# A low-pass image layer on one core: rows and columns streamed together, x read twice

## The chip, the cores and the metric

The kernel runs on one core of a Trainium2 chip. The number that counts is the device time of one execution in microseconds (us). The chip's engines are called PE (TensorE, matmuls), DVE (VectorE), ACT (ScalarE), POOL (GpSimd) and SP (SyncE, which only issues DMAs here). They run side by side, each in the order of its own program, and wait for each other by semaphores.

## What is computed

```python
xs = jnp.einsum('bhwc,dc->bhwd', x, W1) + b1        # x: 16 x 64 x 64 x 768 f32, W1: 192 x 768
xs = jax.nn.gelu(xs, approximate=False)
# fft_low: 2-D FFT over h and w, keep frequencies -16..15 of both, inverse, real part, abs
xs = fft_low(xs)
xs = jnp.einsum('bhwd,cd->bhwc', xs, W2) + b2       # W2: 768 x 192
return x + xs
```

The low pass is a real filter matrix along W, the same along H, and a small correction for the asymmetric frequency, called the corner: it depends on four sums per channel and has period 4 along both axes. Then comes the absolute value.

## The kernel before

Sixteen images pass one after the other. An image has 32 tiles of 128 pixels (two rows each); a *pair* is two tiles, so it has 16 row pairs. A *unit* is four 128x128 blocks of x; a row pair has three units (`UPP`), and a *step* has three parts j = 0, 1, 2.

**Row part of a step** (pair q). PE transposes unit n + 2 (`transpose_unit`, L385), ACT copies it rounded to `xt_hi` (L521), DVE subtracts to `xt_lo` (L640); PE multiplies unit n by W1 (`mm1_unit`, L400 and L401). At j = 1 and j = 2 DVE adds the two PSUM halves and the bias (`hid_sum` L651, `hid_pre` L656). One step later ACT does Gelu twice (L528, L529), DVE the low part (`hid_lo`, L662), PE filters along W (L411 to L413), ACT stages the result in `filt` (L535), and SP writes it to the DRAM tensor `filtered_rows` (L300). POOL accumulates the sums for the corner from `hid` (L760 to L765).

**H phase.** When all rows of an image are written, SP reads them back by columns (L310, L317: pieces of 512 and 256 bytes, into the space of `xt_hi` and `xt_lo`, and into `cols_b`), and PE runs four chunks (`filter_h_chunk`): three banks of 512 columns each, into which first a corner matmul (L435, L443) and then four fp32 filter matmuls (L437, L445) go. ACT and DVE empty the banks with an absolute value into `ya` and `yb` (L543, L680). During the phase no mm1 runs, since its buffers hold the columns.

**Column part of a step** (pair r, of the image before). ACT splits the pair into high parts (`split_hi_pair`, L553 to L559), DVE into low parts (L686, L693), both one step ahead of their use; PE computes four output halves of 384 columns, five matmuls each (`out_half`, L462 to L472), in three PSUM banks in turn; DVE adds each half to x (L702), which has stayed in SBUF as `xs` (the last eight tiles as `x_tail`, copied by ACT, L565). SP stores groups of four tiles and loads the next image's into the freed space (L275 to L295).

**Order.** `steps` sets what runs in a step: in a turn of the loop 8 steps have a column pair alone, 4 have both, 12 have a row pair alone, three more a column pair alone, then follow the H phase and the last column pair. In a column step DVE does `add_half` and the splits after the row part's work of the same j. `turns` writes image 0 out, loops over the rest (`Fori(1, IMAGES)`: 14 jumps back), and ends with the last image's columns. PSUM has eight banks: `ps_xt` 0, 1; `ps_h` 2, 3; `ps_f` 4; `ps_o` 6, 7, 5.

## Time and profile before

| | |
|---|---|
| median of 3 runs | 2669.03 us (2663.34 to 2671.54) |
| the profiled execution, its span | 2680.7 us |
| PE busy | 2549.4 us (95%) |
| DVE busy | 1833.9 us (68%) |
| ACT busy | 1350.4 us (50%) |
| POOL busy | 397.9 us (15%) |
| DMA, mean over the span | 509 MB, 190 GB/s |
| mean granted clock of PE, of full speed | 0.975 |

The rows below come from this one profiled execution. In the table of stretches each row has the stretch in us from the start of the span, its length, then for each engine the time it was busy and (x) how many instructions, the granted PE clock as a share of full speed, the DMA engines' busy share, and GB/s. In the timelines a row has the start in us, the duration in us, engine, line, operation, what is written <- what is read, shapes, how many such instructions are merged (x), and in brackets the idle time ahead of it with what ended it. PE is pipelined: the next matmul starts before the record of the last one ends, so spacings are read from start to start. fp32 matmuls leave two records each.

### The profile page before, as it was taken

Reading aid. Unit: us, or ns where it says so; the run is one execution under the profiler, and the core shown is the slowest. Engines: PE = TensorE matmul, PEld = TensorE weight load, DVE = VectorE, ACT = ScalarE, POOL = GpSimd, SP = SyncE. Lnnn points to the kernel's source line nnn. Section 1 sums busy time; section 2 is a strip of 40 time slices with the busy share of each in tenths; the row PEclk is TensorE's granted clock in tenths of the full one; section 3 lists DMA queues with packets and bytes.
Section 4 is the critical chain, followed back from the end, with each engine's and each line's share of the span. In section 5 each row is a group of like instructions: output and inputs, shape, how many; then the busy total and the mean of one; then the engine's idle time right before and its main releaser. Section 6 shows DMA issues by size and latency. Waiting matters only on the chain.

```text
span 2680.7 us, 53277 instructions
## 1 busy us (share of the span) xinstructions
PE 2549.4 (95%) x16864; PEld 2485.4 (93%) x16864; DVE 1833.9 (68%) x3980; ACT 1350.4 (50%) x3077; POOL 397.9 (15%) x500
## 2 busy tenths in 40 slices
PE   8899898998999989899998999989999899998999
PEld 7799898998989989899898999989999899998999
DVE  6487575775758757587675766757667576675767
ACT  5355454554545545455454545545455454554544
POOL 1102021020211202112020120201202012020120
PEclk9899999999999999999999999999999999999999
DMA  6474664746647466474665846558455584555845
GB/s 207 106 252 138 201 242 114 264 129 200 240 114 261 131 198 242 114 273 129 204 230 129 282 116 215 208 135 298 103 211 202 140 300 99 207 204 145 299 102 221
DMA packets 342566, 509.48 MB, mean 190 GB/s; under 512 B 78418, under 2 KB 210770, under 8 KB 342228
## 3 DMA queue, kind: packets, MB, share of 16 engines
q1 hardware_dynamic: 342228, 505.31, 59.8%
q8 instruction: 171, 2.80, 0.4%
q14 instruction: 167, 1.37, 0.2%
HBM read 253.60 MB, written 251.66 MB: 188 GB/s over the span
## 4 chain that ended last, share of the span: by engine, by line
PE 83%; DMA 6%; SPq 4%; issue 3%; DVE 2%; ACT 2%; DVEq 0%; ACTq 0%
PE ps L400 22%; PE ps L385 12%; PE ps L401 10%; PE ps L472 6%; PE ps L462 6%; PE ps L463 5%; PE ps L469 5%; PE ps L466 5%; DMA xt_hi<-filtered_rows 4%; PE ps L437 3%; SPq L317 2%; PE ps L411 2%; PE ps L445 2%; DMA filtered_rows<-filt 2%; PE ps L413 2%
## 5 line engine op out<-in xcount | busy, mean ns | idle before, releaser
L400 PE MATMUL ps<-w1s,xt_hi 128*128 128x384 f32 x3072 | 980.2, 374 | 0.0
L521 ACT ACTIVATE xt_hi<-ps 128x512 fp32r<-128x512 f32 x768 | 457.7, 598 | 697.8 <-PE ps L385 674.5
L401 PE MATMUL ps<-w1s,xt_lo 128*128 128x192 f32 x3072 | 772.3, 251 | 0.0
L640 DVE TENSOR_TENSOR xt_lo<-ps,xt_hi 128x512 fp32r<-128x512 f32 x768 | 529.8, 691 | 282.4 <-ACT xt_hi L521 279.6
L702 DVE TENSOR_TENSOR xs<-ps,xs 128x384 f32<-128x384 f32 x1024 | 564.5, 556 | 210.9 <-PE ps L472 159.8
L401 PEld LDWEIGHTS ps<-w1s,xt_lo 128*128 128x128 f32 x3072 | 588.0, 191 | 0.0
L400 PEld LDWEIGHTS ps<-w1s,xt_hi 128*128 128x128 f32 x3072 | 578.8, 188 | 0.0
L472 PE MATMUL ps<-w2b_hi,ob 128*128 128x384 f32 x1024 | 357.0, 349 | 42.7 <-DVE ob L693 42.7
L763 POOL TENSOR_TENSOR diff<-hid 128x192 f32<-128x192 f32 x240 | 232.2, 967 | 1016.8 <-ACT hid L529 1016.8
L462 PE MATMUL ps<-w2a_hi,oa_hi 128*128 128x384 f32 x1024 | 361.3, 353 | 20.8 <-DVE xs L702 19.7
L385 PE MATMUL ps<-ident,xs 128*128 128x128 f32 x2304 | 344.1, 273 | 11.2 <-DMA xs<-x_dram 10.6
L463 PE MATMUL ps<-w2a_lo,oa_hi 128*128 128x384 f32 x1024 | 352.7, 344 | 0.0
L466 PE MATMUL ps<-w2b_lo,ob 128*128 128x384 f32 x1024 | 351.7, 343 | 0.6 <-ACT ob L559 0.6
L469 PE MATMUL ps<-w2a_hi,oa_lo 128*128 128x384 f32 x1024 | 352.2, 344 | 0.0
L385 PEld LDWEIGHTS ps<-ident,xs 128*128 128x128 f32 x2304 | 274.6, 140 | 23.3 <-issue 7.6
L472 PEld LDWEIGHTS ps<-w2b_hi,ob 128*128 128x128 f32 x1024 | 197.7, 193 | 56.0 <-DVE ob L693 51.8
L553 ACT ACTIVATE oa_hi<-ya 128x256 fp32r<-128x256 f32 x256 | 106.1, 414 | 279.0 <-PE ps L472 276.9
L462 PEld LDWEIGHTS ps<-w2a_hi,oa_hi 128*128 128x128 f32 x1024 | 197.7, 193 | 31.2 <-issue 29.0
L680 DVE TENSOR_SCALAR ya<-ps 128x512 int32<-128x512 int32 x64 | 44.3, 692 | 234.2 <-PE ps L437 234.2
L466 PEld LDWEIGHTS ps<-w2b_lo,ob 128*128 128x128 f32 x1024 | 198.0, 193 | 1.0 <-ACT ob L559 0.9
L463 PEld LDWEIGHTS ps<-w2a_lo,oa_hi 128*128 128x128 f32 x1024 | 198.2, 194 | 0.2
L469 PEld LDWEIGHTS ps<-w2a_hi,oa_lo 128*128 128x128 f32 x1024 | 197.6, 193 | 0.2
(62 smaller groups left out, 3051.3 us busy)
## 6 DMA issues: line engine op xcount, KB each, us to landing
out_dram<-xs SPq DMA_DIRECT2D x127, 1536.0 KB, 9.3
xs<-x_dram SPq DMA_DIRECT2D x80, 1536.0 KB, 7.2
filtered_rows<-filt SPq DMA_DIRECT2D x256, 192.0 KB, 2.0
x_tail<-x_dram SPq DMA_DIRECT2D x32, 1536.0 KB, 8.5
xs<-x_dram SPq DMA_DIRECT2D x32, 768.0 KB, 6.3
xt_hi<-filtered_rows SPq DMA_DIRECT2D x64, 256.0 KB, 5.1
cols_b<-filtered_rows SPq DMA_DIRECT2D x128, 128.0 KB, 5.4
xt_lo<-filtered_rows SPq DMA_DIRECT2D x64, 256.0 KB, 6.4
```

The costliest lines, as they stand in the source:

```text
L385: ins = nc.tensor.transpose(ps_xt[n % 2][:, b * P:(b + 1) * P], x_tile(t)[:, k * P:(k + 1) * P], ident[:])
L400: nc.tensor.matmul(ps_h[t % 2][:, 0:2 * D], hi, w1s[:, k, :], start=k == 0, stop=False)
L401: ins = nc.tensor.matmul(ps_h[t % 2][:, D:2 * D], lo, w1s[:, k, 0:D], start=False, stop=k == KC - 1)
L462: nc.tensor.matmul(o, a_hi, w2a_hi[:, n], start=True, stop=False)
L463: nc.tensor.matmul(o, a_hi, w2a_lo[:, n], start=False, stop=False)
L466: nc.tensor.matmul(o, b1, w2b_lo[:, n], start=False, stop=False)
L469: nc.tensor.matmul(o, a_lo, w2a_hi[:, n], start=False, stop=False)
L472: nc.tensor.matmul(o, b, w2b_hi[:, n], start=False, stop=True).then_inc(s_o, 1)
L521: nc.scalar.activation(xt_hi[:, n % XT_SLOTS, :], ps_xt[n % 2][:], ACT.Copy).then_inc(s_xhi, 1)
L640: nc.vector.tensor_tensor(xt_lo[:, n % XT_SLOTS, :], ps_xt[n % 2][:], xt_hi[:, n % XT_SLOTS, :].bitcast(F32), ALU.subtract).then_inc(s_xlo, 1)
L702: nc.vector.tensor_tensor(x_half, out_bank(u)[:, 0:HALF], x_half, ALU.add).then_inc(s_add, 1)
L763: nc.gpsimd.tensor_tensor(diff[:], hid[:, q % 2, 0, :], hid[:, q % 2, 1, :], ALU.subtract).then_inc(s_diff, 1)
```

## The change

x is no longer kept in SBUF. It is loaded twice: by row pairs into `xa` (four slots, loaded three steps ahead) for the row part, and by column pairs into `xc` (eight slots, four steps ahead) for the addition and the store; output is stored per column pair. A *column pair* is two positions w, each with all 64 h of both halves of W, so 128 pixels a column. `filtered_rows` has room for all images and is read in eight groups of four columns (`read_cols`, 3072 bytes a piece). Global step s does row pair s, and the column pair whose output halves come 19 steps later (`OUT`); filter H, `y_pair` and the splits of a column pair are done one step ahead of its output halves (`FILTER_H` = 18). There is no H phase any more. The corner is a 128x24 table (three tiny matmuls once per image into the filter's bank, copied by DVE) which `y_pair` adds, repeated along H, when it empties the bank; ACT then takes the absolute value six times: high parts as before, and `y_abs` for the low parts. POOL packs the 64 rear channels of the columns into `cols_b` in every second step. `ps_o` has two banks, 6 and 7. The loop is `Fori(2, IMAGES - 1)`: 12 jumps back.

The core of the diff (of the functions that only got other names for their arguments nothing is shown):

```diff
+PAIRS = 16
...
+AHEAD = 2
 XT_SLOTS = 4
+XA_SLOTS, XA_LEAD = 4, 3
+XC_SLOTS, XC_LEAD = 8, 4
+CHUNKS, COL_SLOTS = 8, 4
+LATE = 1
+FILTER_H = PAIRS + 2
+OUT = FILTER_H + 1
+STORE = OUT + 1
+READ_COLS = FILTER_H - 1
...
+        def stage(i, s, lag):
+            k, r = divmod(s - lag, PAIRS)
+            if whole(i) and not 0 <= i + k < IMAGES:
+                return None
+            return i + k, r
...
+            turn(0, PAIRS)
+            turn(1, PAIRS)
+            with eng.Fori(2, IMAGES - 1) as i:
+                turn(i, PAIRS)
+            turn(IMAGES - 1, PAIRS)
+            turn(IMAGES, PAIRS)
+            turn(IMAGES + 1, STORE - PAIRS)
...
+                    if at := stage(i, s, -XA_LEAD):
+                        load_xa(*at)
+                    if at := stage(i, s, STORE):
+                        store(*at)
+                    if (at := stage(i, s, READ_COLS)) and at[1] == 0:
+                        all_rows_written(at[0])
+                    if at := stage(i, s, OUT - XC_LEAD):
+                        load_xc(*at)
+                    if (at := stage(i, s, READ_COLS)) and at[1] % 2 == 0:
+                        read_cols(at[0], at[1] // 2)
+                    if at := stage(i, s, LATE):
+                        write_rows(*at)
...
+            def filter_h_pair(m, r):
+                c = r // 2
+                if r % 2 == 0:
+                    until(pe, s_cols[c % COL_SLOTS], 16 * CHUNKS // COL_SLOTS, m, 16 * (c // COL_SLOTS + 1))
+                    until(pe, s_cols_b, CHUNKS, m, c + 1)
+                until(pe, s_y, PAIRS, m, r)
+                if r == 0:
+                    until(pe, s_corner, 1, m, 1)
+                col = cols[:, c % COL_SLOTS, 2 * (r % 2):2 * (r % 2) + 2, :]
+                for v in range(2):
+                    nc.tensor.matmul(ps_y[:, v * P:(v + 1) * P], col[:, v, 0:P], fh[:], start=v == 0, stop=False)
+                col_b = cols_b[:, c % COL_SLOTS, 2 * (r % 2):2 * (r % 2) + 2, :].rearrange("p v d -> p (v d)")
+                nc.tensor.matmul(ps_y[:, 2 * P:3 * P], col_b, fh[:], start=False, stop=True).then_inc(s_h, 1)
+            def out_half(m, r, u):
+                v, f = divmod(u, 2)
+                until(pe, s_add, 4 * PAIRS, m, 4 * r + u - 1)
+                o = ps_o[u % 2][:, 0:HALF]
...
+                a_hi, a_lo, b, b1h = (t[:, r % 2, v, :] for t in (oa_hi, oa_lo, ob, ob1))
+                if u == 0:
+                    until(pe, s_hi, PAIRS, m, r + 1)
...
+                if u == 0:
+                    until(pe, s_alo, PAIRS, m, r + 1)
...
+                if u == 0:
+                    until(pe, s_blo, PAIRS, m, r + 1)
...
+                        if at := stage(i, s, 0):
+                            transpose_unit(at[0], UPP * at[1] + j + AHEAD)
+                            mm1_unit(at[0], UPP * at[1] + j)
+                        if j == 1 and (at := stage(i, s, LATE)):
+                            filter_w_pair(*at)
+                        if j == 2 and (at := stage(i, s, FILTER_H - 1)) and at[1] == 0:
+                            corner_sums(at[0])
+                        if at := stage(i, s, OUT):
                             for u in OUT_HALVES[j]:
...
+            def split_hi_pair(m, r):
+                until(act, s_o, 4 * PAIRS, m, 4 * (r - 1))
+                until(act, s_y, PAIRS, m, r + 1)
+                until(act, s_blo, PAIRS, m, r - 1)
+                yr, hi, hi1 = y[:, r % 2, :, :], ob[:, r % 2, :, :], ob1[:, r % 2, :, :]
+                nc.scalar.activation(oa_hi[:, r % 2, :, :], yr[:, 0:2, :], ACT.Abs)
+                nc.scalar.activation(hi[0:DB, 0, :], yr[0:DB, 2, :], ACT.Abs)
+                nc.scalar.activation(hi[DB:P, 1, :], yr[DB:P, 2, :], ACT.Abs)
+                nc.scalar.activation(hi1[0:DB, 0, :], yr[0:DB, 2, :], ACT.Abs)
+                nc.scalar.activation(hi1[0:DB, 1, :], yr[DB:P, 2, :], ACT.Abs)
+                nc.scalar.activation(y_abs[:, r % 2, :, :], yr, ACT.Abs).then_inc(s_hi, 1)
...
+                        if j == 1 and (at := stage(i, s, FILTER_H)):
+                            split_hi_pair(*at)
...
+                until(dve, s_y, PAIRS, m, 0)
+                nc.vector.tensor_copy(corner[:].rearrange("p g n -> p (g n)"), ps_corner[:]).then_inc(s_corner, 1)
+            def y_pair(m, r):
+                until(dve, s_h, PAIRS, m, r + 1)
+                until(dve, s_blo, PAIRS, m, r - 1)
+                if r == 0:
+                    until(dve, s_corner, 1, m, 1)
+                table = corner[:].rearrange("p g (a n) -> p g a n", a=1).to_broadcast([P, 3, 16, 8])
+                nc.vector.tensor_tensor(y[:, r % 2, :, :].rearrange("p g (a n) -> p g a n", n=8),
+                                        ps_y[:, 0:3 * P].rearrange("p (g a n) -> p g a n", g=3, n=8), table,
+                                        ALU.add if r % 2 == 0 else ALU.subtract).then_inc(s_y, 1)
+            def split_lo_pair(m, r):
+                until(dve, s_hi, PAIRS, m, r + 1)
+                yr, hi, o = y_abs[:, r % 2, :, :], oa_hi[:, r % 2, :, :], ob[:, r % 2, :, :]
+                nc.vector.tensor_tensor(oa_lo[:, r % 2, :, :], yr[:, 0:2, :], hi.bitcast(F32), ALU.subtract).then_inc(s_alo, 1)
                 for v, (own, other) in enumerate(((slice(0, DB), slice(DB, P)), (slice(DB, P), slice(0, DB)))):
+                    ins = nc.vector.tensor_tensor(o[other, v, :], yr[own, 2, :], o[own, v, :].bitcast(F32), ALU.subtract)
                 ins.then_inc(s_blo, 1)
+            def add_half(m, r, u):
+                until(dve, s_o, 4 * PAIRS, m, 4 * r + u + 1)
+                n = r % XC_SLOTS
+                if u == 0:
+                    until(dve, s_xc[n], 16 * PAIRS // XC_SLOTS, m, 16 * (r // XC_SLOTS + 1))
+                x_half = xc[:, n, u // 2, u % 2 * HALF:(u % 2 + 1) * HALF]
+                nc.vector.tensor_tensor(x_half, ps_o[u % 2][:, 0:HALF], x_half, ALU.add).then_inc(s_add, 1)
...
+                        if at := stage(i, s, 0):
+                            xt_lo_unit(at[0], UPP * at[1] + j + AHEAD)
+                        if j == 0 and (at := stage(i, s, LATE)):
+                            hid_lo_pair(*at)
+                        if j >= 1 and (at := stage(i, s, 0)):
+                            hid_sum(at[0], 2 * at[1] + j - 1)
+                            hid_pre(at[0], 2 * at[1] + j - 1)
+                        if whole(i) and i == 0 and (s, j) in set_up_at:
+                            set_up_at[s, j]()
+                        if j == 2 and (at := stage(i, s, FILTER_H - 1)) and at[1] == 0:
+                            corner_copy(at[0])
+                        if at := stage(i, s, FILTER_H):
+                            if j == 1:
+                                y_pair(*at)
+                            if j == 2:
+                                split_lo_pair(*at)
+                        if at := stage(i, s, OUT):
+                            for u in OUT_HALVES[j]:
+                                add_half(*at, u)
...
+            def corner_pair(m, q, packs):
+                pool.wait_ge(s_gelu, PAIRS * m + q + 1)
+                if q == 0:
+                    until(pool, s_cmm, 1, m, 0)
+                    if packs:
+                        wait_to_pack(*packs)
+                    nc.gpsimd.tensor_tensor(corner_acc[:], hid[:, 0, 0, :], hid[:, 0, 1, :], ALU.subtract).then_inc(s_acc, 1)
                     return
+                pool.wait_ge(s_acc, PAIRS * m + q)
+                nc.gpsimd.tensor_tensor(diff[:], hid[:, q % 2, 0, :], hid[:, q % 2, 1, :], ALU.subtract).then_inc(s_diff, 1)
+                if packs:
+                    wait_to_pack(*packs)
+                pool.wait_ge(s_diff, (PAIRS - 1) * m + q)
+                nc.gpsimd.tensor_tensor(corner_acc[:], corner_acc[:], diff[:], ALU.add).then_inc(s_acc, 1)
...
+            def pack_cols_b(m, c):
+                n = c % COL_SLOTS
+                nc.gpsimd.tensor_copy(cols_b[:, n, :, :], cols[:, n, :, P:D]).then_inc(s_cols_b, 1)
```

**DVE, j = 1 and the start of j = 2 of a full step.** `ps` are PSUM banks; ISA and REGISTER_ALU rows are waits and their values. Before:

```order
L640 TENSOR_TENSOR xt_lo<-ps,xt_hi 128x512
L650 ISA
L651 TENSOR_TENSOR hid<-ps,b_rows 128x192
L654 ISA
L656 TENSOR_TENSOR hid<-ps,hid 128x192
L697 REGISTER_ALU
L702 TENSOR_TENSOR xs<-ps,xs 128x384
L693 TENSOR_TENSOR ob<-yb,ob 64x8x16 x2
L639 REGISTER_ALU
L640 TENSOR_TENSOR xt_lo<-ps,xt_hi 128x512
```

After:

```order
L493 TENSOR_TENSOR y<-ps,corner 128x384
L152 REGISTER_ALU
L511 TENSOR_TENSOR xc<-ps,xc 128x384
L152 REGISTER_ALU
L459 TENSOR_TENSOR xt_lo<-ps,xt_hi 128x512
L468 TENSOR_TENSOR hid<-ps,b_rows 128x192
L152 REGISTER_ALU
L473 TENSOR_TENSOR hid<-ps,hid 128x192
L500 TENSOR_TENSOR oa_lo<-y_abs,oa_hi 128x256
L502 TENSOR_TENSOR ob<-y_abs,ob 64x128 x2
L152 REGISTER_ALU
L511 TENSOR_TENSOR xc<-ps,xc 128x384
```

`y_pair` (L493) has come in right behind the `hid_pre` of j = 1 (another L473, not shown), and the whole low split (L500, L502) now stands behind the `hid_pre` of j = 2, ahead of the adds of halves 2 and 3; before, it was spread over j = 0 and j = 1.

**ACT, the high split.** Before, it follows the Gelu of j = 0:

```order
L528 ACTIVATE hid_hi<-hid 128x384
L529 ACTIVATE hid<-hid 128x384
L552 REGISTER_ALU
L553 ACTIVATE oa_hi<-ya 128x256
L556 ACTIVATE ob<-yb 64x8x16
L557 ACTIVATE ob<-yb 64x8x16
L558 ACTIVATE ob<-yb 64x8x16
L559 ACTIVATE ob<-yb 64x8x16
L518 REGISTER_ALU
L521 ACTIVATE xt_hi<-ps 128x512
```

After, it stands between `xt_hi` of j = 1 and `xt_hi` of j = 2:

```order
L371 ACTIVATE xt_hi<-ps 128x512
L152 REGISTER_ALU x3
L391 ACTIVATE oa_hi<-y 128x256
L392 ACTIVATE ob<-y 64x128
L393 ACTIVATE ob<-y 64x128
L394 ACTIVATE ob<-y 64x128
L395 ACTIVATE ob<-y 64x128
L396 ACTIVATE y_abs<-y 128x384
L152 REGISTER_ALU
L371 ACTIVATE xt_hi<-ps 128x512
```

It has one instruction more, reads what `y_pair` wrote in the same step, and its successor on ACT is `xt_hi` of the next unit.

## Rows read from the trace of the kernel before

**Rows 1.** Table of stretches: one image; H phase; column steps; full steps; row steps.
```profile
937.70:1105.10 167.40, 159.71 (x1056) 155.92 (x1055) 114.02 (x248) 84.20 (x192) 24.93 (x31) 0.97 0.61 190
937.70:957.29 19.59, 16.61 (x110) 15.61 (x109) 3.90 (x7) 4.18 (x7) 0.00 (x0) 0.83 0.99 197
978.30:992.22 13.92, 13.92 (x82) 13.82 (x81) 12.38 (x29) 12.51 (x28) 0.00 (x0) 1.00 0.81 287
1005.92:1023.49 17.57, 17.57 (x120) 17.36 (x119) 13.55 (x30) 9.11 (x23) 2.67 (x3) 1.00 0.75 252
1058.35:1079.30 20.95, 20.95 (x158) 20.80 (x157) 15.51 (x32) 12.01 (x26) 6.29 (x8) 1.00 0.12 39
```

**Rows 2.** Timeline of DVE just behind the loop's jump back.
```profile
968.94 0.56 DVE L702 TENSOR_TENSOR xs<-ps,xs 128x384 f32<-128x384 f32 x1 [3.39 <-issue]
```

**Rows 3.** Who waited for whom: us in total, times, longest.
```profile
DVE xs L702 <- issue: 40.8, 12, 3.6
PE ps L472 <- DVE ob L693: 42.7, 14, 3.6
```

**Rows 4.** Table of stretches: a wait of PE of 1.24 us; after a long wait.
```profile
961.02:966.70 5.68, 4.44 (x25) 4.12 (x24) 2.23 (x5) 2.19 (x8) 0.00 (x0) 1.00 0.68 262
970.70:974.10 3.40, 3.40 (x13) 3.40 (x12) 1.82 (x5) 0.00 (x0) 0.00 (x0) 0.50 0.00 0
```

**Rows 5.** Timeline of PE: start after a wait; a bank of the H phase.
```profile
962.26 0.44 PE L462 MATMUL ps<-w2a_hi,oa_hi 128*128 128x384 f32 x1 [1.24 <-DVE xs L702]
...
950.88 1.05 PE L437 MATMUL ps<-fh,xt_lo 128*128 128x128 f32 x8
951.69 0.47 PE L435 MATMUL ps<-corner_hw,corner 128*128 128x512 f32 x1
```

**Rows 6.** Timeline of PE in a full step: out half, then transposes.
```profile
1012.54 0.36 PE L462 MATMUL ps<-w2a_hi,oa_hi 128*128 128x384 f32 x1
...
1013.44 0.60 PE L385 MATMUL ps<-ident,xs 128*128 128x128 f32 x4
```

**Rows 7.** Timeline of ACT: in full steps, and a high split with its successor.
```profile
1014.08 0.60 ACT L521 ACTIVATE xt_hi<-ps 128x512 fp32r<-128x512 f32 x1 [1.48 <-PE ps L385]
...
1006.36 0.51 ACT L529 ACTIVATE hid<-hid 128x384 f32<-128x384 f32 x1
1006.77 0.40 ACT L553 ACTIVATE oa_hi<-ya 128x256 fp32r<-128x256 f32 x1
...
978.30 0.42 ACT L553 ACTIVATE oa_hi<-ya 128x256 fp32r<-128x256 f32 x1 [1.89 <-PE ps L472]
...
979.92 0.85 ACT L565 ACTIVATE xs<-x_tail 128x768 f32<-128x768 f32 x1
```

**Rows 8.** Timeline of DVE: two places in full steps, and a low split.
```profile
1014.71 0.69 DVE L640 TENSOR_TENSOR xt_lo<-ps,xt_hi 128x512 fp32r<-128x512 f32 x1 [0.51 <-ACT xt_hi L521]
...
1012.39 0.69 DVE L640 TENSOR_TENSOR xt_lo<-ps,xt_hi 128x512 fp32r<-128x512 f32 x1
1013.00 0.35 DVE L651 TENSOR_TENSOR hid<-ps,b_rows 128x192 f32<-128x192 f32 x1
1013.38 0.36 DVE L656 TENSOR_TENSOR hid<-ps,hid 128x192 f32<-128x192 f32 x1
1013.65 0.55 DVE L702 TENSOR_TENSOR xs<-ps,xs 128x384 f32<-128x384 f32 x1
...
959.80 0.41 DVE L686 TENSOR_TENSOR oa_lo<-ya,oa_hi 128x256 fp32r<-128x256 f32 x1
960.25 0.59 DVE L693 TENSOR_TENSOR ob<-yb,ob 64x128 fp32r<-64x128 f32 x2
960.87 0.56 DVE L702 TENSOR_TENSOR xs<-ps,xs 128x384 f32<-128x384 f32 x1
```

**Rows 9.** Timeline of PE at the start of the span: the first mm1.
```profile
10.94 0.67 PE L400 MATMUL ps<-w1s,xt_hi 128*128 128x384 f32 x1
```

**Rows 10.** The page's costliest groups: busy us, mean ns of one, idle before.
```profile
L763 POOL TENSOR_TENSOR diff<-hid 128x192 f32<-128x192 f32 x240 | 232.2, 967 | 1016.8 <-ACT hid L529 1016.8
```

More of the change, by code:

```diff
@@ L107, in lowpass_kernel @@
         filt = sb("filt", [P, 2, 2, D])
-        x_tail = sb("x_tail", [P, TAIL, C])
-        cols_a = [m[:].bitcast(F32).rearrange("p s (m d) -> p (s m) d", d=P) for m in (xt_hi, xt_lo)]
-        cols_b = sb("cols_b", [P, BCOLS, 2 * DB])
         diff = sb("diff", [P, D])
         corner_acc = sb("corner_acc", [P, D])
-        corner = sb("corner", [P, 2 * P], F32R)
-        ya = sb("ya", [P, TILES, P])
-        yb = sb("yb", [P, 2 * H, BCOLS])
+        corner = sb("corner", [P, 3, 8])
+        y = sb("y", [P, 2, 3, P])
+        y_abs = sb("y_abs", [P, 2, 3, P])
         oa_hi = sb("oa_hi", [P, 2, 2, P], F32R)
@@ L191, in yb_pair @@
-        def yb_pair(r):
-            return yb[:, 8 * r:8 * (r + 1), :]
-        def later(i):
-            return not isinstance(i, int) or i > 0
-        def steps(a, c):
-            if not a:
-                return [(None, r) for r in range(PAIRS)]
-            if not c:
-                return [(q, None) for q in range(PAIRS + 1)]
-            before = PAIRS - TAIL_PAIRS
-            return ([(s - LAG if s >= LAG else None, s) for s in range(before)]
-                    + [(q, None) for q in range(before - LAG, PAIRS)]
-                    + [(PAIRS, before)] + [(None, r) for r in range(before + 1, PAIRS - 1)])
@@ new lines, in turn @@
+            def turn(i, count):
+                for s in range(count):
+                    if whole(i) and i == 0 and s == 0:
+                        const(ident[:], identity, s_ident)
+                        load_xa(0, 0)
+                        const(w1f, w1t.rearrange("(k p) d -> p k d", p=P), s_w1)
+                        load_xa(0, 1)
+                        const(b1_rows[:], b1.partition_broadcast(P), s_b1_rows)
+                        load_xa(0, 2)
+                        load_constants()
+                    if at := stage(i, s, -XA_LEAD):
[10 more added lines that the diff above has]
+                        write_rows(*at)
@@ L361, in _ @@
+            turns(sp, turn)
+            for n in range(XC_SLOTS):
+                sp.wait_ge(s_stored[n], 16 * PAIRS // XC_SLOTS * IMAGES)
         @block.tensor
@@ L582, in turn @@
[L582 to L591 removed]
+                                xt_hi_unit(0, n)
@@ L640, in xt_lo_unit, with hid_sum @@
                 nc.vector.tensor_tensor(xt_lo[:, n % XT_SLOTS, :], ps_xt[n % 2][:], xt_hi[:, n % XT_SLOTS, :].bitcast(F32),
                                         ALU.subtract).then_inc(s_xlo, 1)
-            def hid_sum(i, t):
-                dve.wait_ge(s_m1, UNITS * i + -(-KC * (t + 1) // BLOCKS))
-                if t == 0 and not later(i):
+            def hid_sum(m, t):
+                until(dve, s_m1, UNITS, m, -(-KC * (t + 1) // BLOCKS))
+                if whole(m) and m == 0 and t == 0:
@@ L705, in turn @@
+            def turn(i, count):
                 set_up_at = {(0, 2): set_up_filters, (1, 2): set_up_w2, (3, 2): set_up_w2a_lo, (4, 2): set_up_w2b_lo,
-                             (5, 2): set_up_b2_hi, (6, 2): set_up_b2_lo, (7, 2): set_up_b2_lo_rest}
-                plan = steps(a, c)
-                for s, (q, r) in enumerate(plan):
+                             (5, 2): set_up_b2_hi, (6, 2): set_up_b2_lo}
+                for s in range(count):
                     for j in range(UPP):
-                        if starts(a, c, s, j):
+                        if whole(i) and i == 0 and s == 0 and j == 0:
```

601 lines of the change are left out of this document (178 added, 423 removed).

## The prediction

> **What bounds the kernel now.** I read first the table of stretches, cut at recurring starts of one instruction so that each row is a whole number of steps [rows 1]. TensorE is busy through all of every stretch that is made of steps: a step with a column pair alone takes 13.92 / 4 = 3.48 us, one with a row pair alone 20.95 / 4 = 5.24 us, one with both 17.57 / 2 = 8.79 us. 3.48 + 5.24 is 8.72, so both together cost hardly more than their sum, and in such a step nobody but TensorE is late: VectorE is busy 13.55 of 17.57 us. Only the phase that filters along H holds TensorE up: 19.59 us per image with 16.61 busy, the granted clock at 0.83 and the DMA engines at 0.99. One image takes 167.4 us, and this is its account: 12 column steps (41.8), 4 with both (35.1), 12 row steps (62.9), the H phase (19.6), together 159.4; the other 8 us lie at the loop's end. There VectorE waits "issue" 3.39 us for nothing that the profile shows [rows 2], 12 such waits in all cost it 40.8 us, and TensorE waits for VectorE's `ob` behind it [rows 3]; in the stretch after, its clock is 0.50 [rows 4].
>
> **What the change does to TensorE's work.** Removed: 12 corner matmuls of 512 columns per image and all waiting of the H phase. Moved: the 48 fp32 filter matmuls, now three at a time. Four of them start within 951.69 - 950.88 = 0.81 us [rows 5], so three cost 0.61 and, with the switch of type, 0.69. The three small corner matmuls fall in a place with slack (below). If TensorE stayed the only bound, a full step would be 8.79 + 0.69 = 9.47 us.
>
> **The circle of waits in a full step.** That needs VectorE and ScalarE to keep up in the order written. They are not too busy, but they are chained. `y_pair` stands on VectorE behind `hid_pre` of j = 1, so it waits for the second mm1 unit although filter H is long done; ScalarE's six Abs wait for `y_pair`, and they stand ahead of `xt_hi` of j = 2; VectorE's `xt_lo` of j = 2 waits for that, and behind it stand `hid_sum`, `hid_pre`, `oa_lo`, two `ob` and the adds; the next step's first out half needs add 2 (two banks instead of three) and the splits; behind it stand filter H and the transposes of j = 1, from which the circle starts again. I add it from start to start, with the spacings of the same kinds of instructions:
>
> - transposes to `xt_hi` 1014.08 - 1013.44 = 0.64 [rows 6, 7], to `xt_lo` 0.63, to `hid_sum` 0.61, to `hid_pre` 0.38, to the next instruction 0.27 [rows 8]: 2.53
> - `y_pair`: the trace has none; nearest is the add of 128x384 from PSUM and SBUF, 0.56 [rows 8]. It could be no shorter than the 128x192 form (0.35) and, if the repeated table reads slowly, twice 0.56: 0.35 to 1.12, taken 0.56, since size and sources are the same. With 0.04 to ScalarE: 0.60
> - ScalarE, five instructions of the same shapes as now: 979.92 - 978.30 = 1.62; `y_abs` 128x384 to the next 1006.77 - 1006.36 = 0.41; `xt_hi` to `xt_lo` 0.63 [rows 7, 8]: 2.66
> - VectorE: 0.61, 0.38, 0.27, `oa_lo` to `ob` 0.45, `ob` pair to add 0.62, the add itself 0.56 and 0.05 to TensorE [rows 8]: 2.94
> - TensorE: out half 1013.44 - 1012.54 = 0.90 [rows 6], 0.10 more for a start after a wait (the first record is 0.44 long [rows 5]), filter H 0.69: 1.69
>
> Sum 2.53 + 0.60 + 2.66 + 2.94 + 1.69 = **10.42 us**. TensorE does 9.47 of work in it and waits 0.95 ahead of each step's first out half. Its other work fits: VectorE's adds 0 and 1, `hid_lo` and ScalarE's Gelu and staging lie in gaps of the circle, and the corner matmuls (j = 2) lie ahead of the wait, which swallows them. Sixteen full steps are then 166.7 us, what an image takes now: the change gives back in steps what it saves in the phase. From both sides: each of the 13 edges is good to about 0.05, and `y_pair` adds -0.2 to +0.56, so 9.9 to 11.0 per step with 9.47 as floor.
>
> **The sum**, for one profiled execution. 237 steps are full (row pairs 19 to 255 with column pairs 0 to 236), 19 have rows alone, 19 columns alone.
> - Start to the first mm1: 11 [rows 9], and 4 for early waits
> - 19 row steps x 5.24 = 100
> - 237 x 10.42 = 2470
> - 19 column steps. Here the circle is out half 1.00, filter H 0.69, its last record's end 0.28 later, `y_pair` 0.60, Abs 1.62 + 0.51, splits 0.45 + 0.62, add 0.61: 6.4 us for 4.2 us of work. TensorE idles a third of the time, so I add 0.5 for stretches at the lower clock: 6.9 x 19 = 131 (bounds 4.2 and 9)
> - corner copy on VectorE inside the circle, 0.3 x 16 = 5
> - loop end: 12 jumps back instead of 14. Now one costs 8 us; a full step asks VectorE for fewer instructions per microsecond, and part of the wait falls in gaps it has anyway. Bounds 0 and 6, taken 2.5: 30
> - last add and store: 6
>
> Together 2757. The profiled execution of before is 2680.7 against a median of 2669.0, 11.7 less; so **2745 us**, 2.8% slower.
>
> The Trainium skill (Runtime: NRT & Kernel Launch, "Instruction fetch mechanics") says that a taken branch whose target is outside the fetched window must wait for a DMA before it goes on. The waits of [rows 2] agree in place. If the fetch itself were the whole price, the 3.4 us would be paid by 12 jumps, 41 instead of 30, and the total would be 2756.
>
> **DMA and Pool.** x is read twice: per step 0.79 MB each for rows, columns and output, 0.2 each for writing and reading filtered rows, 2.75 MB. The column steps move 287 GB/s at a share of 0.81 [rows 1], so 354 at full; 2.75 MB take 7.8 of 10.4 us, a share of 0.75, with loads issued three and four steps ahead. Hidden; the cover is gone below 7.8 us per step. The tightest transfer is `cols`: issued behind store and xc (together 1.97 MB, 5.6 us), packed by Pool (nearest row 0.97 us for 192 columns [rows 10], so 0.6 to 1.9 for 256), needed by filter H about 10 us after the store's issue. One to two us of slack.
>
> **Rivals.**
> 1. *TensorE stays the bound* (some edge of the circle does not bind): 237 x 0.95 = 225 less, and some 30 less at the end: 2490. For it: full steps now show no wait at all. Against: they have three banks, and splits a whole step ahead.
> 2. *The circle binds, but shorter*, near 9.95: 237 x 0.47 = 111 less, 2634. The edges are spacings under load, and some could overlap.
> 3. *The clock falls.* A single wait of 1.24 us left it at 1.00, the one of 3.47 was followed by 0.50 [rows 4]. If 0.95 in every step were enough now and then, each fall would cost 1.7 us (3.4 at half rate); every second step: +200, 2945. The Trainium skill (TensorE: Matmul & The Clock Gate, "The HAM clock gate") says that activity releases the throttle, which goes with this rival.
> 4. *`cols` or the packing comes late*: Pool's accumulation stands behind the wait for `cols`, `hid_sum` behind that, filter H behind both. 1.2 us over the slack in every second step: 118 x 1.2 = 142, 2887.
>
> The side is decided at one point: the other terms make 287, so (2680.7 - 287) / 237 = 10.10 us per full step is break-even.
>
> **Chances.** My forecast 0.56 (own range 2690 to 2800), rival 1 0.13, rival 2 0.16, rival 3 0.07, rival 4 0.08. Rival 2 and the lower edge of the forecast hold the break-even, so within 0.3% (8 us, about what a measurement of this kernel tells from no change) 0.06; faster 0.26, slower 0.68. The range leaves out rivals 1 and 3 and takes in 2 and 4: 2590 to 2900.
>
> **What the profile after would show.** Full steps of 10.4 us between Gelu starts; TensorE idle 0.9 to 1.0 ahead of L324, released by VectorE's L511; `y_pair` L493 starting 0.3 after L473 and ScalarE's L391 released by it; clock near 1.00; DMA share near 0.75; column steps at the end of 6.4 to 7 us. I am wrong if L324 shows no wait (rival 1), if full steps run at a clock below 0.95 (rival 3), or if filter H or Pool wait for `cols` (rival 4).

## The result and the profile after

The changed kernel takes 2814.51 us (median of 4 runs, 2805.99 to 2830.43), the kernel before beside it 2670.28. The ratio is 1.055, 95% interval 1.051 to 1.060: 5.5% slower, where 2745 us had been forecast. The profiled execution has a span of 2810.3 us. The page of the kernel after, engines with busy time, share and instructions, then the main DMA queue:

```profile
PE 2524.1 (90%) x16736; PEld 2437.7 (87%) x16736; DVE 1872.8 (67%) x4123; ACT 1274.3 (45%) x3076; POOL 359.8 (13%) x628
...
q1 hardware_dynamic: 233236, 706.40, 72.7%
```

No engine is full: TensorE, busy through every stretch of steps in [rows 1], is idle for a tenth of the span at a mean granted clock of 0.991. The table of waits (us in total, times, longest) says before what:

```profile
POOL corner_acc L558 <- DMA cols<-filtered_rows: 933.1, 105, 11.0
...
DVE xt_lo L459 <- ACT xt_hi L371: 795.4, 518, 6.3
...
ACT oa_hi L391 <- DVE y L493: 347.3, 180, 2.5
...
PE ps L324 <- DVE xc L511: 220.9, 243, 1.8
...
ACT xt_hi L371 <- issue: 37.6, 5, 8.5
PE ps L265 <- issue: 35.4, 12, 3.6
...
PE ps L312 <- DMA cols<-filtered_rows: 2.8, 2, 2.0
```

TensorE waits 220.9 us for VectorE's adds, ahead of L324, the first matmul of an out half: 225 of the 243 waits, 190.4 us, fall in the 237 full steps; ScalarE waits in the other direction, for `y_pair` (L493). VectorE's waits "issue" of [rows 3] are down to 2.3 us: at the jump it is now ScalarE and TensorE that wait for nothing the profile shows. The stretch of two full steps, and the last 131 us (us, busy of PE, PEld, DVE, ACT, POOL with counts, clock, DMA share, GB/s), answer to [rows 1]:

```profile
1343.22:1364.40 21.18, 19.41 (x132) 18.83 (x131) 14.59 (x33) 9.91 (x26) 2.97 (x6) 1.00 0.76 261
...
2675.00:2806.00 131.00, 95.10 (x506) 84.08 (x504) 71.27 (x157) 39.42 (x114) 5.61 (x12) 0.95 0.66 235
```

One full step can be followed around on its timeline (start, duration, idle before and who ended it). First VectorE and ScalarE, then TensorE's two out halves 0, one step apart:

```profile
1366.08 0.43 PE L324 MATMUL ps<-w2a_hi,oa_hi 128*128 128x384 f32 x1 [1.09 <-DVE xc L511]
...
1367.72 0.60 PE L265 MATMUL ps<-ident,xa 128*128 128x128 f32 x4
...
1368.36 0.60 ACT L371 ACTIVATE xt_hi<-ps 128x512 fp32r<-128x512 f32 x1 [3.04 <-PE ps L265]
...
1368.99 0.69 DVE L459 TENSOR_TENSOR xt_lo<-ps,xt_hi 128x512 fp32r<-128x512 f32 x1 [1.04 <-ACT xt_hi L371]
...
1370.26 0.55 DVE L493 TENSOR_TENSOR y<-ps,corner 128x384 f32<-128x384 f32 x1
...
1370.84 0.42 ACT L391 ACTIVATE oa_hi<-y 128x256 fp32r<-128x256 f32 x1 [1.88 <-DVE y L493]
...
1372.43 0.53 ACT L396 ACTIVATE y_abs<-y 128x384 f32<-128x384 f32 x1
...
1372.86 0.58 ACT L371 ACTIVATE xt_hi<-ps 128x512 fp32r<-128x512 f32 x1
...
1373.48 0.69 DVE L459 TENSOR_TENSOR xt_lo<-ps,xt_hi 128x512 fp32r<-128x512 f32 x1 [2.00 <-ACT xt_hi L371]
...
1375.81 1.02 DVE L511 TENSOR_TENSOR xc<-ps,xc 128x384 f32<-128x384 f32 x2
...
1376.49 0.44 PE L324 MATMUL ps<-w2a_hi,oa_hi 128*128 128x384 f32 x1 [0.71 <-DVE xc L511]
```

From 1366.08 to 1376.49 it is 10.41 us, and each start stands directly behind its predecessor in the circle: transposes (L265) to `y_pair` 2.54, to ScalarE 0.58, its five operations 1.59, `y_abs` to `xt_hi` 0.43, to `xt_lo` 0.62, to the add 2.33, to TensorE 0.68, out half and filter H 1.64.

But not every step takes that. The starts of Gelu (L377) are a clock for the steps: 10.77, 10.41, 10.79. Beside each stands VectorE's `ob` pair (L502), and where Pool works at that moment, what it does:

```profile
1343.22 0.52 ACT L377 ACTIVATE hid_hi<-hid 128x384 fp32r<-128x384 f32 x1
1343.22 0.94 DVE L502 TENSOR_TENSOR ob<-y_abs,ob 64x128 fp32r<-64x128 f32 x2
1343.42 0.59 POOL L558 TENSOR_TENSOR corner_acc<-corner_acc,diff 128x192 f32<-128x192 f32 x1 [9.11 <-DMA cols<-filtered_rows]
...
1353.98 0.59 DVE L502 TENSOR_TENSOR ob<-y_abs,ob 64x128 fp32r<-64x128 f32 x2
1353.99 0.52 ACT L377 ACTIVATE hid_hi<-hid 128x384 fp32r<-128x384 f32 x1
...
1364.17 0.64 POOL L558 TENSOR_TENSOR corner_acc<-corner_acc,diff 128x192 f32<-128x192 f32 x1 [8.58 <-DMA cols<-filtered_rows]
...
1364.38 0.98 DVE L502 TENSOR_TENSOR ob<-y_abs,ob 64x128 fp32r<-64x128 f32 x2
1364.40 0.52 ACT L377 ACTIVATE hid_hi<-hid 128x384 fp32r<-128x384 f32 x1
...
1375.19 0.58 DVE L502 TENSOR_TENSOR ob<-y_abs,ob 64x128 fp32r<-64x128 f32 x2
1375.19 0.52 ACT L377 ACTIVATE hid_hi<-hid 128x384 fp32r<-128x384 f32 x1
```

Where Pool's corner sum is in flight, the pair takes 0.94 and 0.98 instead of 0.59 and the step is 0.36 to 0.38 longer. That was not in the forecast. Between the 19th Gelu and the last lie the 237 full steps, 2553.8 us, or 87 more than 237 x 10.41. The experiments divide these 87 us.

### The profile page after: what moved, and what is told of

Read it like the earlier page. It is cut to its first block and busy times, and to the rows that moved or that the text cites. A ratio compares the mean times of both kernels' runs of the same rounds, so it can differ in the third digit from the quotient of the medians.

```text
span 2810.3 us, 55293 instructions
## 1 busy us (share of the span) xinstructions
PE 2524.1 (90%) x16736; PEld 2437.7 (87%) x16736; DVE 1872.8 (67%) x4123; ACT 1274.3 (45%) x3076; POOL 359.8 (13%) x628
## 5 line engine op out<-in xcount | busy, mean ns | idle before, releaser
L511 DVE TENSOR_TENSOR xc<-ps,xc 128x384 f32<-128x384 f32 x1024 | 545.7, 554 | 58.0 <-PE ps L332 27.4
L324 PE MATMUL ps<-w2a_hi,oa_hi 128*128 128x384 f32 x1024 | 382.5, 374 | 220.9 <-DVE xc L511 220.9
L265 PE MATMUL ps<-ident,xa 128*128 128x128 f32 x3072 | 464.3, 274 | 43.8 <-issue 35.4
L324 PEld LDWEIGHTS ps<-w2a_hi,oa_hi 128*128 128x128 f32 x1024 | 193.7, 189 | 279.5 <-issue 211.4
L265 PEld LDWEIGHTS ps<-ident,xa 128*128 128x128 f32 x3072 | 375.9, 141 | 64.4 <-issue 45.1
L391 ACT ACTIVATE oa_hi<-y 128x256 fp32r<-128x256 f32 x256 | 106.8, 417 | 547.8 <-DVE y L493 347.3
L332 PE MATMUL ps<-w2b_hi,ob 128*128 128x384 f32 x1024 | 347.6, 339 | 0.2 <-DVE ob L502 0.2
L554 POOL TENSOR_TENSOR diff<-hid 128x192 f32<-128x192 f32 x240 | 151.7, 632 | 1110.1 <-ACT hid L378 1108.7
L558 POOL TENSOR_TENSOR corner_acc<-corner_acc,diff 128x192 f32<-128x192 f32 x240 | 149.7, 624 | 943.7 <-DMA cols<-filtered_rows 933.1
L473 DVE TENSOR_TENSOR hid<-ps,hid 128x192 f32<-128x192 f32 x512 | 183.1, 358 | 17.6
```

The lines of the kernel that those rows point to most:

```text
L265: ins = nc.tensor.transpose(ps_xt[n % 2][:, b * P:(b + 1) * P], src, ident[:])
L324: nc.tensor.matmul(o, a_hi, w2a_hi[:, n], start=True, stop=False)
L332: nc.tensor.matmul(o, b, w2b_hi[:, n], start=False, stop=True).then_inc(s_o, 1)
L473: nc.vector.tensor_tensor(h, ps_h[t % 2][:, 0:D], h, ALU.add).then_inc(s_pre, 1)
L511: nc.vector.tensor_tensor(x_half, ps_o[u % 2][:, 0:HALF], x_half, ALU.add).then_inc(s_add, 1)
```

## Experiments

Times stand beside 7 runs of the kernel before on the same chip (medians 2669 to 2677); "the changed kernel" is 2814.51 throughout, from four executions that lie 24 us apart, so a difference of 10 us from it says little. The theory is the circle of waits; its rivals are those of the prediction.

**One part of the circle taken out.** On VectorE only:

```diff
-                        if at := stage(i, s, FILTER_H):
-                            if j == 1:
-                                y_pair(*at)
-                            if j == 2:
-                                split_lo_pair(*at)
+                        if j == 2 and (at := stage(i, s, FILTER_H)):
+                            split_lo_pair(*at)
                         if at := stage(i, s, OUT):
                             for u in OUT_HALVES[j]:
                                 add_half(*at, u)
+                        if j == 0 and (at := stage(i, s, FILTER_H)):
+                            y_pair(*at)
```

> The changed kernel, with one move: VectorE adds the corner (y_pair) at the end of unit j=0, right behind add 0, instead of in unit j=1 behind the second sum. ScalarE's five Abs stay where they are, in j=1. Theory (the circle of waits sets the full step): the path from the filter over H through y_pair to ScalarE no longer waits for VectorE's transposed split and its two sums, so the circle is shorter than TensorE's own 9.47 us and a full step goes from 10.41 to about 9.5: 237 x 0.94 = 223 us less, about 2590 us. Rival A (TensorE's own work or its clock is the bound, and the wait ahead of out half 0 only fills up): no change, 2814. Rival B (VectorE, now waiting for the filter over H in the middle of j=0, is late for the transposed split of j=1, and the circle only closes elsewhere): half of it, about 2700.

Measured: 2583.42 us, ratio to the kernel before 0.967 (0.964 to 0.969). Two full steps of it:

```profile
1397.79:1416.72 18.93, 18.93 (x132) 18.79 (x131) 14.94 (x32) 9.91 (x25) 4.40 (x7) 1.00 0.83 294
```

TensorE is busy 18.93 of 18.93 us, 9.47 per step: its own work, as the prediction had it without the circle. One instruction moved ahead by one unit makes the change 3.3% faster instead of 5.5% slower, so neither the second read of x nor the corner's addition itself costs the steps anything there.

**One link doubled**, into a buffer that nobody reads:

```diff
+                nc.vector.tensor_tensor(y_spare[:, r % 2, :, :].rearrange("p g (a n) -> p g a n", n=8),
+                                        ps_y[:, 0:3 * P].rearrange("p (g a n) -> p g a n", g=3, n=8), table,
+                                        ALU.add if r % 2 == 0 else ALU.subtract)
```

> The changed kernel, with y_pair's addition issued twice, first into a spare buffer that nobody reads. Theory (y_pair lies on the circle of waits, and nothing in it has slack): each full step gets longer by the second addition, 0.45 to 0.55 us, so 237 x 0.5 = 119 us and as much on the last column steps (19 x 0.5 = 9): about 2940 us. Rival (TensorE bound, VectorE is 67% busy and has room): no change, 2814.

Measured: 2932.9 us, 118 more. The undisturbed steps take 10.87, 0.46 more, which is what lies from start to start between the two additions. The timeline shows the link that grew:

```profile
1429.34 0.55 DVE L494 TENSOR_TENSOR y_spare<-ps,corner 128x384 f32<-128x384 f32 x1
1429.80 0.55 DVE L497 TENSOR_TENSOR y<-ps,corner 128x384 f32<-128x384 f32 x1
1430.38 0.42 ACT L392 ACTIVATE oa_hi<-y 128x256 fp32r<-128x256 f32 x1 [2.34 <-DVE y L497]
```

VectorE is busy 67% of the span and still passes on all of it. That, with the run before it, shows the circle.

**ScalarE's part moved away instead**: `split_hi_pair` in unit j = 2 (`if j == 1` becomes `if j == 2`, behind `xt_hi`).

> The changed kernel, with ScalarE's five Abs (split_hi_pair) moved from unit j=1 to unit j=2, behind that unit's transposed copy. Theory: they no longer stand between the corner's addition and the transposed copy that VectorE and TensorE need next, the circle loses about 1 us, and a full step falls to what TensorE takes or a little above, 9.5 to 9.8 us: 150 to 215 us less, 2600 to 2665. Rival (the wait only moves: out half 0 of the next step then waits for the low parts, which VectorE makes later): between 2750 and 2850.

Measured: 2714.86 us, 100 less, only half of what the theory gave and between its range and the rival's. The undisturbed steps are as expected, 9.66 to 9.67; but others take 10.2 to 11.0, and in the waits stands a new name:

```profile
PE ps L312 <- POOL cols_b L568: 54.4, 54, 1.8
```

Filter H (L312) waits for the packed columns, 54 times; in the kernel after it did so once, 1.1 us. It is the mechanism of rival 4. With `y_pair` early it hardly happens, though the steps are shorter still: 9 weight loads wait for Pool there, 6.6 us in all. So the length of the step alone does not bring it on, and what does in this order was not tested.

**Is it Pool beside VectorE?** First the packing alone, cut to one element (`cols_b[:, n, 0:1, 0:1]`):

> The changed kernel, where the Pool engine's packing copies one element per chunk instead of the rear 64 channels of four columns; those channels of the filter over H are left out of the computation (TensorE still does its matmuls on zeros). Theory: every second step of the changed kernel is 0.3 to 0.7 us longer than 10.41 because VectorE's subtractions of two SBUF operands take longer while Pool reads and writes SBUF; without the packing half or more of that goes: 20 to 40 us less, about 2780. Rival (the longer steps come from DMA queues or a missing buffer, not from Pool): no change, 2814.

Measured: 2805.28 us (2803.93 to 2813.73), 9 less, below what was expected and near what the runs can tell. The corner sum (L558 of the kernel after) still starts where it did, since it stands behind the same wait. So the next run took all of Pool's operations to one element:

```diff
-                nc.gpsimd.tensor_tensor(corner_acc[:], corner_acc[:], diff[:], ALU.add).then_inc(s_acc, 1)
+                nc.gpsimd.tensor_tensor(corner_acc[:, 0:1], corner_acc[:, 0:1], diff[:, 0:1], ALU.add).then_inc(s_acc, 1)
```

> The changed kernel, where each of Pool's operations (difference, corner sum, packing) takes one element per partition instead of 192 or 256; the corner and the rear 64 channels of the filter over H are left out of the computation, and every wait, every DMA and all other work stay. With a quarter of the second read the time fell to 2751 us and the odd steps to 10.41, though the share of DMA at 0.75 left room. Theory (the DMA of the columns only sets when Pool starts its corner sum and its packing; those lengthen VectorE's subtractions of SBUF operands on the circle): with Pool idle and all of the DMA there, the odd steps go to 10.41 too, 2745 to 2765 us. Rival (the transfers themselves, or the descriptors of DMA, lengthen the steps): above 2795, as without the packing alone (2805).

Measured: 2779.99 us, 34.5 less; the theory's lower steps came (10.41 in odd and even ones), its total did not, by 15. The groups of the `ob` pair (busy us, mean ns, idle before), of the kernel after and of this one:

```profile
L502 DVE TENSOR_TENSOR ob<-y_abs,ob 64x128 fp32r<-64x128 f32 x512 | 173.1, 338 | 11.4
```
```profile
L503 DVE TENSOR_TENSOR ob<-y_abs,ob 64x128 fp32r<-64x128 f32 x512 | 147.1, 287 | 11.5
```

VectorE's pair gets 26 us back, and the 237 steps shrink by 24 us (2530.1 against 2553.8).

**What remains of 87 us: the second read, and the jumps.** Three quarters of the second read left out from the second image on:

```diff
+                if whole(m) and m == 0:
                     sp.dma_start(xc[:, n, :, :], x_cols[m, :, 2 * r:2 * r + 2, :]).then_inc(s_xc[n], 16)
+                else:
+                    sp.dma_start(xc[:, n, 0:1, 0:HALF], x_cols[m, :, 2 * r:2 * r + 1, 0:HALF]).then_inc(s_xc[n], 16)
```

> The changed kernel, where from the second image on the second read of x brings only one quarter of a column pair (half the channels of one column of the two); the residual that is added is stale for the rest, which leaves that part of x out of the output. It takes 0.56 MB of the 2.75 MB that a full step moves. Theory (DMA at a share of 0.75 is not what a full step waits for): 2814, within 0.3%. Rival (queueing behind the second read delays the loads of rows, the columns or the stores, and the reread of x is what makes the changed kernel slower): more than 30 us less, and all of the 144 us if nothing else made it slower, 2670.

Measured: 2751.22 us, 63 less, on the rival's side. This is the largest miss of the study: "hidden" was wrong, though no engine ever waited for `xc`. Two things changed. First, the columns land earlier behind less traffic, so Pool starts earlier. The issue of `cols` on SP's queue in the kernel after, whose row of Pool's sum at 1364.17 stands above, and then both in this one:

```profile
1356.80 0.82 SPq L212 DMA_DIRECT2D cols<-filtered_rows  x1
```
```profile
1496.97 0.84 SPq L215 DMA_DIRECT2D cols<-filtered_rows  x1
...
1501.79 0.60 POOL L561 TENSOR_TENSOR corner_acc<-corner_acc,diff 128x192 f32<-128x192 f32 x1 [6.05 <-DMA cols<-filtered_rows]
```

From issue to sum 7.4 us there, 4.8 here: Pool's work has left the moment in which VectorE makes `ob`, whose mean falls to 290 ns. In the kernel after, 74 of Pool's 105 sums that wait for `cols` start within 0.6 us of the `ob` pair's start; here it is 4. Second, the jumps got cheaper. Compared with Pool idle, where the steps are as even, a turn of the loop takes 168.7 instead of 172.1 us (means of the 12 with a jump, from Gelu to Gelu), and TensorE's wait at the jump is shorter:

```profile
PE ps L268 <- issue: 19.9, 12, 2.2
```

It was 35.4 us for the same 12 in the kernel after (L265). The other part is the clock, right behind the jump. The first stretch is of the kernel after, where TensorE had waited 2.8 us, the second of this run, where it had waited 1.4:

```profile
1126.20:1129.40 3.20, 3.20 (x13) 3.20 (x14) 0.25 (x1) 0.00 (x0) 0.00 (x0) 0.50 1.02 393
```
```profile
767.00:770.30 3.30, 3.30 (x26) 3.30 (x27) 1.90 (x5) 1.42 (x3) 0.01 (x1) 1.00 0.84 271
```

In the full steps of the kernel after, the granted clock is 0.50 behind ten of the twelve jumps, for 37.5 us in all; with Pool idle behind eleven, 54.6 us; in this run behind three, 10.2 us. As half of such time is lost at most, that is up to 19, 27 and 5 us (an estimate). Between this run and Pool idle lie 12 x 3.3 = 40 us, to which TensorE's shorter waits give 15 and the clock up to 22. So a jump is cheaper with less traffic; why the wait itself is shorter, this one comparison does not show. The Trainium skill (Runtime: NRT & Kernel Launch, "Instruction fetch mechanics") has a taken branch wait for a DMA fetch of its target, where that lies outside the fetched window. The page of the profile agrees in so far as the two instruction queues bring 337 packets (4.11 MB) in the kernel after and 228 (2.97 MB) with all turns written out, the next run; but that program also executes fewer instructions (46,665 against 55,293), and nothing here ties a fetch to a wait.

**No jumps**: all turns written out (`for i in range(IMAGES + 1)` in place of the loop), of the changed kernel and of the one before.

> The changed kernel with the instructions of all 17 turns written out, so that no engine jumps. Theory (each of the loop's 12 jumps puts about 5 us on the circle: the three steps around it take 36.2 us in the profile where three others take 31.4): 12 x 4.8 = 58 us less, about 2757. Rival A (the prediction's 2.5 us per jump): 30 less, 2785. Rival B (the instructions have to be fetched anyway, and a straight program waits for them as long): no change, 2814.

> The kernel before with its loop's turns written out. It says how much of the difference of 144 us lies in jumps rather than in steps: the kernel before drains at each jump, as its image's last steps wait for each other. Theory: 14 jumps, 5 to 7 us each, 70 to 100 us less, 2570 to 2600. Rival (the jump is hidden under the drained image end): under 20 us less, above 2650.

Measured: 2760.03 us, 54.5 less or 4.5 per jump, the theory and not the prediction's 2.5; and 2567.3 us for the kernel before, 103.5 less or 7.4 for each of its 14. Without jumps the change is therefore 193 us slower, not 144: it had made the jumps fewer and cheaper (54.5 against 103.5 us in all), and the circle's 0.94 us in each of 237 steps, 223 us, is more than the whole of the 193. These prices hold the clock too: the kernel before runs at a granted clock of 0.50 for 138.5 us, behind its jumps and in its H phases, and for 23.0 with its turns written out, which is up to 58 of the 103.5 us (an estimate).

**Both**: `y_pair` early and no jumps.

> y_pair early, as in the run with that one move (2583 us), and no loop either. Theory: the steps stay at 9.47 us and TensorE never waits for a jump, and the two gains add up: 2583 less 12 x 4 to 5 us is 2520 to 2535. Rival (with a TensorE bound step, buffers run ahead and hide most of the jump already): above 2560.

Measured: 2507.27 us, 76 less than with the loop, more than expected: a jump costs 6.3 us in this order and 4.5 in that of the kernel after. A likely reason, not tested, is that every wait counts where TensorE is the bound, while the circle leaves it 0.94 per step to swallow some of it.

**The last 19 steps.** With the rest at TensorE's own pace, these stand out: 6.33 us in some, 7.0 to 9.2 in others, for about 4.5 us of TensorE's work. Filter H ahead of out half 0, and `y_pair` ahead of add 0, in all steps:

> y_pair early and no loop (2507 us), and in unit j=0 the filter over H now comes ahead of out half 0 on TensorE, and y_pair ahead of add 0 on VectorE. Theory: full steps stay at 9.47 us, TensorE's own work; the 19 column steps at the end lose out half 0 and its add (1.7 us) from their circle and go from about 7 us to about 5: 30 to 40 us less, 2467 to 2477. Rival (the column steps are bound by the transfers of 1.73 MB per step, or the full steps lose what they had, since VectorE now waits for the filter over H): 2500 or more.

Measured: 2528.51 us, 21 more; the rival. Some 15 of the 21 us lie in the full steps (2264.3 us for the 237, and 2249.6 in the run before it): most still take 9.47, but some 9.6 to 10.4 and one 13.5, and TensorE waits ahead of filter H 16 times there, 7.3 us in all. In the last steps the columns are issued one step ahead, and the shorter steps outran them: most of them take 5 to 6 us and 8 to 11 in turn. The timeline there:

```profile
2428.51 0.91 SPq L208 DMA_DIRECT2D cols<-filtered_rows  x1
...
2434.66 0.40 POOL L563 COPY cols_b<-cols 128x256 f32<-128x256 f32 x1 [13.89 <-DMA cols<-filtered_rows]
2435.16 1.10 PE L308 MATMUL ps<-fh,cols 128*128 128x128 f32 x4 [4.08 <-DMA cols<-filtered_rows]
```

After 4.08 us of waiting the four matmuls take 1.10 instead of 0.60: the clock has fallen as well. (The 10.0 us at each image's first columns are no cost of this order: the run before it, in the old order, has 14 such steps too.) So the reads of `cols` were put one chunk ahead, first with the old order:

```diff
                     if (at := stage(i, s, READ_COLS)) and at[1] % 2 == 0:
-                        read_cols(at[0], at[1] // 2)
+                        if at[1] == 0:
+                            read_cols(at[0], 0)
+                        if at[1] // 2 + 1 < CHUNKS:
+                            read_cols(at[0], at[1] // 2 + 1)
```

> y_pair early and no loop (2507 us), and the read of each chunk of columns is issued one chunk (two steps) earlier: chunks 0 and 1 together, then one ahead; the filter over H stays behind out half 0. Theory: of the last 19 steps, every second one takes 7.0 to 9.2 us instead of 6.33 because its columns, issued one step before, land 6 us later; with the reads ahead they all take 6.33: 9 x about 1.2 = 11 us less, about 2496. Rival (the reads then delay the loads of x in the full steps): above 2507.

Measured: 2504.35 us, 3 less instead of 11. The wait for the columns is gone (0.5 us in all), and still every second or third step takes 7.1 to 7.7. Two stretches of one step each:

```profile
2408.75:2415.07 6.32, 4.49 (x28) 4.08 (x27) 3.69 (x8) 2.07 (x6) 0.40 (x1) 1.00 0.88 308
2415.07:2422.71 7.64, 5.82 (x27) 5.40 (x26) 3.69 (x8) 2.07 (x7) 0.00 (x0) 0.78 0.78 248
```

The same work takes TensorE 5.82 instead of 4.49 us at a mean clock of 0.78: the engine waits 1.8 us for add 2 in each of these steps, and in some it comes out of that wait at the half clock. My expectation had one cause for the long steps, the columns; the clock is the other. Last, the short circle where it helps, in the last turn alone:

```diff
+                        if j == 0 and i >= IMAGES and (at := stage(i, s, FILTER_H)):
+                            filter_h_pair(*at)
                         if at := stage(i, s, OUT):
                             for u in OUT_HALVES[j]:
                                 out_half(*at, u)
-                        if j == 0 and (at := stage(i, s, FILTER_H)):
+                        if j == 0 and i < IMAGES and (at := stage(i, s, FILTER_H)):
                             filter_h_pair(*at)
```

> As the run before it, and from the turn of the last column steps on (i = 16) the filter over H stands ahead of out half 0 and y_pair ahead of add 0. With that order everywhere and the columns read late it was 2528 us: TensorE waited 4 to 5 us for the columns in every second of the last steps and then ran at the half clock, and each image's first column pair cost 0.5 us. Theory: with the columns there in time, the last steps take 4.8 to 5.2 us, 16 x 1.2 = 19 us less than the run before it, 2470 to 2485. Rival (the transfers, 1.73 MB per step, 4.9 us at the 353 MB per ms of the full steps, or a clock that falls in the emptier steps, take the place of the wait): 2490 to 2510.

Measured: 2477.98 us, ratio to the kernel before 0.927 (0.924 to 0.931), and 3.5% below that kernel with its loop written out. The 237 full steps are those of the run before it (2248.4 us). Fifteen of the last steps take 4.76 to 4.93 us from out half 0 to out half 0:

```profile
2380.00:2460.00 80.00, 70.89 (x401) 66.20 (x400) 54.69 (x123) 31.61 (x92) 3.20 (x8) 0.96 0.88 327
```

It is the fastest version of this study, with TensorE busy 99% of the span.

## Why the prediction was right, and where its size was off

**What bounds the kernel, and the circle.** Right. The full step was forecast at 10.42 us and an undisturbed one takes 10.41; no edge is off by more than 0.07. TensorE waits ahead of L324 in 225 of the 237 steps, released by L511, by the profile 0.3 to 1.5 us and 0.72 in the median (0.95 forecast, and 10.41 - 9.47 = 0.94 from start to start). `y_pair`, for which the trace of before had no row, took 0.55, the value of the nearest row. Without the circle the forecast was 9.47 per step, and 9.47 was measured. Rivals 1 and 2 are out: in the timeline every link starts right behind its predecessor, and doubling one costs its whole 0.46 us. Rival 3 is out as it was put, since the wait of 1 us in each full step leaves the clock at 1.00; the clock does fall behind ten of the twelve jumps and in the last 19 steps. Rival 4 did not come either, though the sign given for it ("if filter H or Pool wait for `cols`") did: Pool waits 933.1 us for `cols` ahead of its sum (L558), but filter H (L312) only 2.8 us. Pool's wait alone was no sign of it.

**The sum, for the profiled execution**: 2757 forecast, 2810.3 measured, 53 more.
- Up to the 19th Gelu 122.1 us against 115, 7 more: the step ahead of it takes 11.5, and the first filter over H in it waits 3.0. After the last Gelu 134.4 us against 137, 3 less. The 19 column steps at 6.9 were right in size, 6.93 on average; the reason given, the circle of 6.4 (6.33 measured) and stretches at the lower clock, was part of it, another part being columns that land late.
- The full steps and what lies between them: 2470 + 5 + 30 = 2505 forecast, 2553.8 measured, 49 more, though the steps themselves, 237 x 10.41, are 2467. **The jump** is the term that was mis-sized most surely: 12 x 4.5 = 55 instead of 30. The step that failed is "part of the wait falls in gaps it has anyway": [rows 2] shows only VectorE's wait at the jump. In the kernel after, ScalarE waits up to 8.5 us and TensorE 3.6, 35.4 us in all, and whatever waits is a link of the circle, which has no gap. The clock behind the jump adds up to 19 us; [rows 4] showed it at 0.50 there before, and the term did not carry it. The sentence on the fetch as the whole price gave 41, and that is low too.
- **Pool beside VectorE**, 24 us, had no term at all. The step that failed is the last part, "DMA and Pool", which asked only whether the packed columns come in time. They do; but Pool's start, set by the landing of `cols`, falls on the `ob` pair, a link of the circle. A hint stood in [rows 10]: Pool's difference took 967 ns there, and 632 after, so its length depended on what ran beside it.
- The rest, if the two add up, is 87 - 55 - 24 = 8 us against 5 for the corner copy. It goes with what remains with Pool idle between two jumps, where 16 steps take 166.4 to 167.2 us instead of 166.6.

**Profile to median.** 11.7 us were taken off, as the profiled execution of before lay above its median. That of after lies 4.2 below its own. With 53 this makes up the 69 us between 2745 and 2814.5. The result is 14.5 us outside the forecast's own range (2690 to 2800), halfway between the forecast and the time of rival 4 (2887), without the latter's mechanism; that it is inside the wider range (2590 to 2900) owes something to that rival's room. The break-even of 10.10 us per step was too high, since the terms beside the steps came to 2810.3 - 2467 = 343 us and not 287; with them it is 9.86. The step of 10.41 is above both, so the side did not hang on it.

**"x is read twice: hidden."** Hidden from the waits, not from the time: about 63 us less with a quarter of it, through Pool's start and the price of the jumps. The test by share of the DMA (0.75) and by who waits for whom was too coarse.

## What to carry to other kernels

Walk once around the step by the start-to-start spacings of the profile; if that circle is longer than the busiest engine's work, it is the step, and one instruction issued in an earlier place may give back everything. Where a circle binds, any lengthening of a link counts in full: a jump, a second engine at the same memory, a later start of a neighbour. A transfer that nobody waits for can still set when another engine starts, and so whom it disturbs.

## What the runs showed of the hardware

**VectorE and Pool get in each other's way on operands in SBUF, and the one that starts second pays.** In the kernel after, Pool first, then VectorE's subtraction of two SBUF operands:

```profile
1387.88 0.59 POOL L558 TENSOR_TENSOR corner_acc<-corner_acc,diff 128x192 f32<-128x192 f32 x1
1388.02 0.87 DVE L478 TENSOR_TENSOR hid_lo<-hid,hid_hi 128x384 fp32r<-128x384 f32 x1
```

0.87 instead of 0.55: 0.32 more, of the 0.45 that Pool's operation still had to run. In the full step above, the `ob` pair that started at 1364.38 beside Pool's sum took 0.98 instead of 0.59. With `y_pair` early it is the other way round, and Pool's difference takes 0.97 instead of 0.60 beside a VectorE at its usual 0.56:

```profile
1408.22 0.56 DVE L478 TENSOR_TENSOR hid_lo<-hid,hid_hi 128x384 fp32r<-128x384 f32 x1
1408.26 0.97 POOL L553 TENSOR_TENSOR diff<-hid 128x192 f32<-128x192 f32 x1 [7.83 <-ACT hid L378]
```

VectorE's adds with one operand in PSUM keep their 1.02 for two beside Pool's packing (1386.48, with the packing at 1386.85). The Trainium skill (SBUF — State Buffer, "SBUF: two separate sides") describes a port pair that the two engines share, taken for a whole instruction by whichever starts first, and for VectorE only with two inputs in SBUF or in a two-port mode. These rows agree in who pays and which operations do; by that section the second one waits for all that is left of the first, 0.45 and 0.52 us here, and it was 0.32 and 0.37 longer.

**The price of a jump is no constant**: 7.4 us in the kernel before, 4.5 in the one after, 6.3 where TensorE is the bound. It has two parts, the wait and the clock behind it: TensorE's waits of 2.7 to 3.6 us at eleven of the jumps in the kernel after were followed by the half rate ten times, its wait of 1.6 us at the twelfth was not; with a quarter of the second read the waits were 1.2 to 2.2 us and the half rate came three times.

**The clock**: one wait of 1 us in a step of 10.4 left it at 1.00, apart from the stretches behind jumps; in steps of 6.3 with 4.5 us of work it fell to the half rate in every second or third one.
